# Routing in finer batches, sent earlier, and the last batch's rows sent one block per expert slot

## The reference

```python
# x: (4, 1024, 128); everything in float32
x = x + attn_a(layernorm(x))      # linear attention, a causal running state over each sequence
x = x + moe(layernorm(x))         # layer 0's experts
x = x + attn_b(layernorm(x))      # a decayed running sum of x, two projections, sigmoid(r) * mix
x = x + moe(layernorm(x))         # layer 1's experts, the same weights

def moe(x):
    logits = x @ router_W + router_b               # 8 experts
    probs = softmax(logits); top1 = argmax(probs)
    gates = one_hot(top1) * probs
    h = relu(x @ W1[e] + b1[e]); y = h @ W2[e] + b2[e]   # 128 -> 512 -> 128
    return sum_e gates[e] * y[e]
```

## Time and profile before

| | |
|---|---|
| runs | 393.11, 397.33, 392.72 us; median 393.11 |
| profiled execution | 397.11 us, span 395.2 us |
| PE busy | 296.7 us (75% of the span) |
| DVE busy | 250.0 us (63%) |
| POOL busy | 201.3 us (51%) |
| ACT busy | 147.1 us (37%) |
| layer 0: slots, experts | to about 95, then to about 202 us |
| layer 1: slots, experts | to about 283, then to about 387 us |

### The profile page before, as it was taken

The page is one execution under the profiler, slowest core; times in us unless marked ns, Lnnn a source line. Parts: engine busy times, 40 slices in busy tenths (PEclk is TensorE's granted clock), DMA queues, the critical chain, the costliest instruction groups (busy, mean ns, idle before and its releaser), DMA issues.

```text
span 395.2 us, 8901 instructions
## 1 busy us (share of the span) xinstructions
PE 296.7 (75%) x2097; PEld 258.3 (65%) x2097; DVE 250.0 (63%) x996; ACT 147.1 (37%) x413; POOL 201.3 (51%) x259
## 2 busy tenths in 40 slices
PE   2899999680599379999923989695089729999980
PEld 1367666450488279999912878574088629999980
DVE  4656788784388167877725579467248627777760
ACT  3545554211133024444414555724123203444430
POOL 5823517777345724555424152777734554445550
PEclk9999999986589669999985889977559957999996
DMA  7990000024446448876325000001645736877700
GB/s 206 240 165 4 1 2 28 29 56 141 118 129 178 108 113 221 218 209 191 81 76 138 2 0 2 27 27 43 169 136 148 186 66 179 227 205 199 188 19 0
DMA packets 42609, 44.21 MB, mean 112 GB/s; under 512 B 7120, under 2 KB 29905, under 8 KB 42560
## 3 DMA queue, kind: packets, MB, share of 16 engines
q10 hardware_dynamic: 11808, 20.71, 20.9%
q1 hardware_dynamic: 26176, 14.39, 15.7%
q0 software_dynamic: 4576, 8.54, 6.1%
HBM read 33.06 MB, written 11.53 MB: 113 GB/s over the span
## 4 chain that ended last, share of the span: by engine, by line
PE 38%; issue 27%; DVE 11%; SPq 7%; another core or an unknown queue 5%; POOL 5%; ACT 2%; DMA 2%; DVEq 1%; POOLq 0%; ACTq 0%
PE pair L1319 14%; PE pair L1305 11%; PE bank L1305 4%; PE pair L1246 2%; POOL sorted L453 2%; DVE hT L1017 2%; SPq L344 2%; PE pair L1247 2%; SPq L340 2%; PE pair L1264 2%; SPq L312 1%; DVE xsn L1001 1%; ACT xn L535 1%; DVEq L1006 1%
## 5 line engine op out<-in xcount | busy, mean ns | idle before, releaser
L1319 PE MATMUL pair<-w2s,hT 128*128 x624 | 89.0, 289 | 8.2 <-issue 7.6
L1319 PEld LDWEIGHTS pair<-w2s,hT 128*128 128x128 f32 x624 | 80.9, 203 | 10.4 <-issue 9.9
L453 POOL DMA_INDIRECT sorted<-rows,place x64 | 64.2, 1003 | 31.3 <-issue 17.8
L1305 PE MATMUL pair<-xsT,w1s 128*128 128x128 f32 x472 | 70.2, 288 | 0.8 <-issue 0.8
L1305 PEld LDWEIGHTS pair<-xsT,w1s 128*128 128x128 f32 x472 | 63.6, 205 | 1.2 <-issue 1.2
L459 POOL DMA_INDIRECT out<-ys,xs x39 | 38.0, 975 | 41.2 <-issue 26.4
L459 POOL DMA_INDIRECT x_mid<-ys,xs x39 | 38.0, 975 | 40.7 <-issue 23.4
L1017 DVE TENSOR_SCALAR hT<-pair,w1s 128x128 f32<-128x128 f32 x156 | 47.1, 343 | 8.6 <-remote 3.9
L1028 DVE SCALAR_TENSOR_TENSOR ys<-pair,xs 128x128 f32<-128x128 f32 x78 | 27.2, 349 | 25.7 <-remote 13.0
L1009 DVE SCALAR_TENSOR_TENSOR xs<-b2b,xs 128x128 f32<-128x128 f32 x78 | 27.4, 352 | 21.4 <-DVE xsn L1001 14.6
L646 ACT COPY xsT<-bank 128x128 f32<-128x128 f32 x40 | 10.6, 265 | 67.4 <-PE bank L1296 27.4
(11 more groups left out here) (160 smaller groups left out, 505.5 us busy)
## 6 DMA issues: line engine op xcount, KB each, us to landing
w1s<-in_L_ffn_W_b ACTq DMA_DIRECT2D x78, 258.0 KB
xs<-sorted SPq DMA_DIRECT2D x78, 66.0 KB
rows<-in_L_attn_a_x SPq DMA_DIRECT2D x8, 256.0 KB, 4.9
w2s<-in_L_ffn_W SPq DMA_DIRECT2D x8, 256.0 KB, 5.5
rows<-x_mid SPq DMA_DIRECT2D x8, 256.0 KB, 4.8
sorted<-pad SPq DMA_DIRECT2D x30, 66.0 KB, 3.5
sorted<-rows,place POOLq DMA_INDIRECT x64
x_mid<-ys,xs POOLq DMA_INDIRECT x39
```

The source lines that it names most:

```text
L453: pool.indirect_dma_start(sorted_rows[l], bass.IndirectOffsetOnAxis(ap=place[:, t:t + 1], axis=0), rows[:, t, :], None).then_inc(s_sent[l] ...
L1305: mm = nc.tensor.matmul(bank[2 + 2 * half + i % 2][:, c * P:(c + 1) * P], w1s[i % NW][:, f:f + P], xsT[i % NB][:], start=True, stop=True)
L1319: mm = nc.tensor.matmul(bank[6 + i % 2][:, 0:P], hT[i % NB][:, c], w2s[:, bass.ds(e, 1), c, :].rearrange("p o d -> p (o d)"), start=(c == ...
```

## The change

The eight groups' routing batches become `[[0], [1], [2], [3], [4], [5], [6, 7]]` instead of `[[0, 1], [2, 3], [4], [5], [6, 7]]`. The stages keep their slots and their groups and are renumbered. `choose` and `placed` stand earlier in DVE's slot, `lexp` at the end of ACT's, `count` first in PE's mix slot. Each group is sent one slot sooner: at k-4 in place of k-5 in layer 0, in halves around `old_logits`, and at k-3 in place of k-4 in layer 1. The last batch is chosen, counted and placed one or two expert slots sooner, and its eight sends go out one behind each scatter of slots 4 to 11.

```diff
-ROUTE_BATCHES = [[0, 1], [2, 3], [4], [5], [6, 7]]
-STAGES = [(1, 9), (3, 8), (4, 22)]
-CHOOSE_AT, COUNT_AT, TABLE_AT = 3, 6, 6
+ROUTE_BATCHES = [[0], [1], [2], [3], [4], [5], [6, 7]]
+STAGES = [(3, 9), (5, 8), (6, 22)]
+CHOOSE_AT, COUNT_AT, TABLE_AT = 2, 4, 5
 # POOL
+            def send(l, S, g, half=None):
+                if half != 1:
+                    rows_ready(l, S, g)          # the four waits of the old send
+                for t in range(g * GT + (GT // 2 if half == 1 else 0), (g + 1) * GT - (GT // 2 if half == 0 else 0)):
+                    send_tile(l, t)
             def experts(l):
                 for i in range(ST):
                     scatter(l, i)
-                    if i == COUNT_AT - 1:
-                        for g in ROUTE_BATCHES[LASTB]:
-                            send(l, (AS, BS)[l], g)
+                    if i == COUNT_AT:
+                        rows_ready(l, (AS, BS)[l], LASTG)
+                    if COUNT_AT <= i < COUNT_AT + len(late):
+                        send_tile(l, late[i - COUNT_AT])
 # POOL, layer 0's slots
-                if k - 5 >= 0:
-                    send(0, AS, k - 5)
+                if k - 4 >= 0:
+                    send(0, AS, k - 4, 0)
                 if 0 <= k - 1 < NG:
                     old_logits(k - 1)
-            send(0, AS, 4)
+                if k - 4 >= 0:
+                    send(0, AS, k - 4, 1)
             send(0, AS, 5)
 # POOL, layer 1's slots
-                if k - 4 >= 0:
-                    send(1, BS, k - 4)
-            send(1, BS, 5)
+                if k - 3 >= 0:
+                    send(1, BS, k - 3)
 # ACT, layer 1's slots (layer 0's likewise)
-                if (b := batch_ending(ROUTE_BATCHES, k - 3)) is not None and b < LASTB:
-                    lexp(1, BS, b)
                 if 0 <= k - 1 < NG:
                     evac_x2T(k - 1)
+                if (b := batch_ending(ROUTE_BATCHES, k - 2)) is not None and b < LASTB:
+                    lexp(1, BS, b)
```

More of the change, by code:

```diff
@@ L451, in send, with send_tile @@
                 pool.wait_ge(S["place"], b + 1)
[L452 to L454 removed]
+            def send_tile(l, t):
+                b = batch_of(ROUTE_BATCHES, t // GT)
+                pool.indirect_dma_start(sorted_rows[l], bass.IndirectOffsetOnAxis(ap=place[:, t:t + 1], axis=0),
+                                        rows[:, t, :], None).then_inc(s_sent[l][stage_of_batch(b)], 16)
+            def send(l, S, g, half=None):
[3 more added lines that the diff above has]
+                    send_tile(l, t)
             def scatter(l, i):
@@ L464, in experts @@
             def experts(l):
+                late = [t for g in ROUTE_BATCHES[LASTB] for t in range(g * GT, (g + 1) * GT)]
                 for i in range(ST):
                     scatter(l, i)
-                    if i == COUNT_AT - 1:
-                        for g in ROUTE_BATCHES[LASTB]:
-                            send(l, (AS, BS)[l], g)
+                    if i == COUNT_AT:
+                        rows_ready(l, (AS, BS)[l], LASTG)
+                    if COUNT_AT <= i < COUNT_AT + len(late):
+                        send_tile(l, late[i - COUNT_AT])
             def first_indirect():
@@ L609, in attn_slot @@
                     evac_o(k - 1)
-                if k == NG:
-                    lexp(0, AS, LASTB - 1)
+                if (b := batch_ending(ROUTE_BATCHES, k - 3)) is not None and b < LASTB:
+                    lexp(0, AS, b)
             def gates_of_mix(g):
@@ L853, in attn_slot @@
                     mask_scores(k - 1)
+                if (b := batch_ending(ROUTE_BATCHES, k - 4)) is not None and b < LASTB - 1:
+                    placed(0, AS, b)
                 if 0 <= k - 2 < NG:
@@ L857, in attn_slot @@
                     add_state(k - 1)
-                if (b := batch_ending(ROUTE_BATCHES, k - 4)) is not None and b < LASTB - 1:
-                    placed(0, AS, b)
+                if (b := batch_ending(ROUTE_BATCHES, k - 3)) is not None and b < LASTB:
+                    choose(0, AS, b)
                 if 0 <= k - 2 < NG:
@@ L903, in mix_slot @@
                     scan_mix(k + 1)
+                if (b := batch_ending(ROUTE_BATCHES, k - 3)) is not None and b < LASTB:
+                    placed(1, BS, b)
+                if (b := batch_ending(ROUTE_BATCHES, k - 2)) is not None and b < LASTB:
+                    choose(1, BS, b)
                 if 0 <= k - 1 < LASTG:
@@ L908, in mix_slot @@
                     first_moments(1, k + 4)
-                if (b := batch_ending(ROUTE_BATCHES, k - 3)) is not None and b < LASTB:
-                    placed(1, BS, b)
-                if (b := batch_ending(ROUTE_BATCHES, k - 2)) is not None and b < LASTB:
-                    choose(1, BS, b)
                 if k == NG - 1:
@@ L1271, in mix_slot @@
                     transpose_x(BS, k + 1)
+                if (b := batch_ending(ROUTE_BATCHES, k - 3)) is not None and b < LASTB:
+                    count(BS, b, bank[7])
                 if 0 <= k - 2 < NG:
@@ L1275, in mix_slot @@
                     mix(k)
-                if (b := batch_ending(ROUTE_BATCHES, k - 3)) is not None and b < LASTB:
-                    count(BS, b, bank[7])
                 if 0 <= k - 1 < LASTG:
```

6 lines of the change are left out of this document (1 added, 5 removed).

## The result

The changed kernel takes 398.62 us, median of 20 runs (395.26 to 403.33), beside 394.06 for the kernel before (391.40 to 397.33, 20 runs). The ratio is 1.0091, 95% interval 1.0065 to 1.0116: slightly slower, within 2%. (It is taken over the executions in the chip's faster state alone, and so lies a little under the ratio of these medians.) 381 us was forecast, and the range ended at 392. The profiled executions differ more than the medians: they took 402.7 and 397.1 us, with spans of 401.0 and 395.2 us.

A forecast was written before the change was run, and what follows sets the result against it. Largest movable loss: the expert phases' hole, PE's signals held up while POOL issues indirect DMAs and SP issues too. Layer 0's -6.4 and layer 1's -4.6, with about 1 us of clock, made -12: 393.1 to 381 us, range 368 to 392.

The forecast's parts named there:

- Layer 0's slots, +1.3: Layer 0's slots: extra choose and placed +5.1, less waiting behind sends, collisions +2; sum +1.3 us, between -0.7 and +7.
- slot 8, -1.6: Layer 0's slot 8: the 1.65 us that DVE waits for the exponential go, -1.6 us.
- entry, -4.6: Entry into layer 0's experts: earlier loads -3.5, four fewer sends -1.1, together -4.6 us; bounds 0 and -5.6.
- The collisions: Layer 0's slots: DVE blocked beside POOL's product, 0.5 us a slot in four slots, +2; 13 us if every `choose` collides.
- Layer 1's entry, -4.6: Entry into layer 1's experts: exponential a slot earlier and loads starting with slot 8, -4.6 us, between -2 and -7.
- The last batch's hole, -5: Each expert phase: interleaving sends with scatters removes part of the late-signal hole, -5 us a layer, between -11 and 0.
- The rival of vanishing signals: Expert phases: pauses at scatters suffice, so the hole gives 11 us a layer, not 5; 369 us, chance 0.16.
- the one of a longer hold-up: Expert phases: hold-up lasts through all eight interleaved slots, +8 us a layer instead of -5; 407 us, chance 0.10.
- Placing in one slot, +1: Expert slot 3: choosing, counting and placing stand together, so DVE waits once for a count, about +1 us a layer.
- The new wait, +2.5: Before expert slot 14: slot 17's load waits for the last send, +2.5 us a layer, between 0 and +6.
- Layer 1's slots, +1.5: Layer 1's slots: six more table loads against waits for POOL's scales that go, +1.5 us, between -2 and +9.
- the slots eat the gain: More collisions, or table loads fully on the chain and the new wait at its upper end: 393 us, chance 0.22.

The follow-up runs named there:

- the empty ones: Kernel before plus sixteen indirect DMAs with all indices out of bounds, eight in a row in layer 0, one a slot in layer 1: ratio 1.0513.

## Why the prediction was wrong, step by step

- **Layer 0's slots, +1.3; slot 8, -1.6; entry, -4.6: right, if a little low.** `phi` 3 to 7 went from 34.1 to 33.7, and the way to the first `xsn` gained 6.2, as forecast for the last two together. The late `dmax` stayed (6.36 us of "remote", ended 1.4 us after the last of a row of sends). The run with layer 0's slots alone gives them a gain of 2.0%, some 8 us. The collisions, put at 2 us, were few: `ls` took 1.30 and 1.29 us in two of layer 0's six batches (1.33 in one of four before) and no more than 0.19 in all six of layer 1. The version in which every `choose` collides, and the change stands near none for that reason, is excluded.
- **Layer 1's entry, -4.6: right**, 5.0 measured.
- **The last batch's hole, -5: wrong, the step that failed first.** `ys` 4 to 13 went from 31.6 to 29.9 in layer 0 and from 31.6 to 30.6 in layer 1: 1.6 and 1.0 gained. I had taken less than the middle between "nothing lost" and "all lost" because a scatter's wait for its `ys` would make POOL pause. It does pause, and then POOL catches up at 1.27 us a piece, without one. The lower bound, all of it lost, was near the truth: the cost comes from indirect DMAs that follow each other at 1.27 us, be they sends or scatters, and not from the sends standing together. The rival of vanishing signals had the same flaw; the one of a longer hold-up had the mechanism but not its size, since it counted a delay for each slot, where a row of DMAs delays once: three rows here, of four, four and six. Its sign, "remote" idle rows over all of these slots, came in this form.
- (The prediction's arithmetic calls the `ys` at 153.22 slot 12's; it is slot 13's, nine slots behind slot 4, and 155.12 is slot 14's. The step from `ys` 6 to 7 alone has 10.7 us of lateness, so the size of the hole isn't changed by it. But the rival of a longer hold-up had nine slots to count, not eight, and would have come out higher. And the signals came 1.9 us after the last indirect DMA, not 3: the prediction overlooked the scatter behind the sends.)

```profile
136.81 0.99 POOL L459 DMA_INDIRECT x_mid<-ys,xs  x1 [0.30 <-issue]
```

- **Placing in one slot, +1: too small.** `ys` 0 to 4 grew by 3.1 and 3.8 us.
- **The new wait, +2.5: right.** `ys` 13 to 14 grew by 3.0 in layer 0 and by 2.8 in layer 1.
- **Layer 1's slots, +1.5: wrong.** +8.7, at the bound of +9 that I had kept. I had costed the table loads against single slots and expected 8.2 us for each slot from 4 to 8; the slots from 2 on took 9.4, 10.0, 8.9, 10.8, 6.4 and 11.0. Of the 8.7 us, 5.5 are in slots 2 and 3 (+2.6 forecast) and 3.2 in the four after them (-1.1 forecast). I had counted DVE's waits for POOL's scales behind sends as gone; they grew from 4.0 to 6.7 us. What I left out, as I read the rows, is that the batch of one group closes a chain in every slot: POOL's sends and scales, `choose`, count, and the reload ahead of `sg`. The runs show that the batches with their sooner sends cost it, and not which link.

With the measured terms, from the windows: -0.4 -6.2 -0.3 +5.2 in layer 0, +8.7 -5.0 +7.7 in layer 1, and -3.4 at the start, -0.6 between, make +5.7, the difference of the spans (5.8). The experts' +5.2 is 3.1 for placing, -1.6 for the hole, 3.0 for the new wait and 0.7 for the last 24 steps; +7.7 is 3.8, -1.0, 2.8 and 2.1. The two largest misses are the hole (7.4 us in both layers together) and layer 1's slots (7.2). Of the rivals "the slots eat the gain" (393) came nearest in number. Of its causes, collisions were few and the new wait was as forecast, so that leaves layer 1's slots, where the loads' share is open. Both large terms were set from argument at the favourable half of their bounds.

## What to carry to other kernels

Count the indirect DMAs of GpSimd as a resource with its own pace beside the slots, and look at how far apart they are issued. Where a slot of 1.9 us already has one, spreading a burst over slots doesn't hide it. Routing earlier did gain here: layer 0's new slots as a whole, with each group sent a slot sooner, gave 2.0%. Which part of them gives how much wasn't measured. Before making batches smaller in a slot pipeline, write down the longest chain that each batch runs through the engines and ask whether it fits one slot.

## What the hardware showed

PE's signals reach the engines that wait for them up to 11 us late while GpSimd issues indirect DMAs 1.27 to 1.38 us apart, until about 1 to 2 us after the last. At 1.55 us apart it is 0.4 to 1.2 us a slot, and at 1.83 us nothing. It takes no rows moved (the empty ones do it), no DMA of SP, and not a busy GpSimd as such. SP's own issuing is slowed as well (eight pads in 16.59 us beside the row, in 7.26 behind it). In the midst of a row a signal of DVE came in time: its hidden rows of 133.27 ended at 133.88 and PE's product on them began at 134.08. Whether PE's work itself is late or only what it reports, no run tells: PE's pause of 3.58 us above ended 0.2 us after DVE's hidden rows, which had themselves been released late. The Trainium skill, "SBUF — State Buffer", Who interferes with whom, says that "PE and ACT never wait on anyone". It speaks of SBUF ports, and the runs don't tell whether these matter here; for the engines that wait on PE, ACT among them, the measured delays of up to 11 us decide.
